# Attention by two problems side by side instead of one, in an eight-core layer kernel

## What is computed

```python
xn = _layernorm(x, axis=-1)                       # x: (4, 4096, 1024)
# attention: b, s, d = 4, 4096, 1024; H = 16, head size 64
Q = (x @ Wq.T).reshape(H, b, s, dkh)              # the same for K and V
scores = jnp.einsum('hbqd,hbkd->hbqk', Q, K)
atten = jax.nn.softmax(scores, axis=-1)
out = jnp.einsum('hbqk,hbkd->hbqd', atten, V).reshape(b, s, -1)
y = out + x
mu, var = mean and variance of y over (1, 2)      # one pair per batch entry
return (y - mu) / jnp.sqrt(var + EPS)
# mixture of experts on xn: gates are the softmax of the two best of 8 logits
h = xt @ w_in[e].T
y = y + gates[:, e:e + 1] * (h @ w_out[e].T)
# result: x + attention(xn) + experts(xn)
```

## Time and profile before

| quantity | value |
|---|---|
| profiled execution | 5827.74 us |
| span of its slowest core | 5825.9 us |
| all cores | 5811.5 to 5825.9 us |
| PE (TensorE) busy | 4843.9 us, 83% |
| ACT (ScalarE) busy | 2392.6 us, 41% |
| DVE (VectorE) busy | 1389.9 us, 24% |
| POOL busy | 146.4 us, 3% |
| mean granted TensorE clock | 0.864 of 2.4 GHz, the same on all cores |
| chain that ended last | PE 67%, ACT 16%, issue 6%, DMA 5%, DVE 5% |

### The profile page before, as it was taken

The page is one execution under the profiler, slowest core; times in us unless marked ns, Lnnn a source line. Parts: engine busy times, 40 slices in busy tenths (PEclk is TensorE's granted clock), DMA queues, the critical chain, the costliest instruction groups (busy, mean ns, idle before and its releaser), DMA issues.

```text
span 5825.9 us, 62049 instructions; the slowest of 8 cores (5811.5 to 5825.9 us)
## 1 busy us (share of the span) xinstructions
PE 4843.9 (83%) x19844; PEld 1763.2 (30%) x19844; DVE 1389.9 (24%) x3688; ACT 2392.6 (41%) x2339; POOL 146.4 (3%) x290
## 2 busy tenths in 40 slices
PE   1888888888888984888888888888968999999994
PEld 1422222232222113222222222222113444444442
DVE  3211111111111105111111111111024444444445
ACT  1455555565555552555556555555530000000000
POOL 1000000000000000000000000000000000000000
PEclk9988888888898556888898889887559999999997
DMA  5000000000000002000000000000026565677543
GB/s 76 4 1 4 4 1 4 1 4 4 1 4 1 4 1 33 1 4 1 4 1 4 4 1 4 1 4 1 0 40 106 92 93 92 100 116 116 96 81 83
DMA packets 86068, 173.88 MB, mean 30 GB/s; under 512 B 4864, under 2 KB 4864, under 8 KB 85760
## 3 DMA queue, kind: packets, MB, share of 16 engines
q0 software_dynamic: 83456, 161.54, 17.8%
q1 hardware_dynamic: 2304, 8.39, 0.4%
HBM read 323.06 MB, written 8.39 MB: 57 GB/s over the span
## 4 chain that ended last, share of the span: by engine, by line
PE 67%; ACT 16%; issue 6%; DMA 5%; DVE 5%; DVEq 1%; ACTq 1%; POOL 0%; POOLq 0%
PE P_OT L374 17%; PE P_S L426 17%; ACT AR L303 14%; PE P_S L504 11%; PE P_A L352 5%; PE P_B L352 5%; PE P_OT L522 4%; DMA AR<-woutT 4%; PE P_B L522 2%; PE P_A L522 2%; PE P_B L361 1%; DMA xstg<-xb 1%; ACT AR L315 1%; PE P_A L361 1%; DVE gsc L623 1%
## 5 line engine op out<-in xcount | busy, mean ns | idle before, releaser
L303 ACT ACTIVATE AR<-P_S,consts 128x1024 bf16<-128x1024 f32 x2048 | 2254.1, 1114 | 1629.3 <-PE P_S L426 1613.2
L374 PE MATMUL P_OT<-AR 128*65 128x512 bf16 x4096 | 1414.0, 430 | 350.9 <-ACT AR L303 350.6
L426 PE MATMUL P_S<-AR 64*128 64x512 bf16 x4096 | 1452.4, 447 | 3.6 <-DVE AR L547 3.0
L504 PE MATMUL P_S<-AR 128*128 128x512 bf16 x4096 | 891.7, 380 | 19.1 <-DMA AR<-woutT 12.9
L374 PEld LDWEIGHTS P_OT<-AR 128*65 128x65 bf16 x4096 | 312.1, 116 | 1304.0 <-issue 1294.7
L504 PEld LDWEIGHTS P_S<-AR 128*128 128x128 bf16 x4096 | 400.6, 98 | 508.6 <-issue 31.7
L426 PEld LDWEIGHTS P_S<-AR 64*128 64x128 bf16 x4096 | 263.2, 99 | 943.5 <-issue 929.5
L734 DVE TENSOR_TENSOR AR<-P_S,AR 128x512 bf16<-128x512 f32 x384 | 265.6, 692 | 412.5 <-PE P_S L504 412.5
L538 DVE CAST AR<-P_B 64x256 bf16<-64x256 f32 x256 | 106.7, 417 | 978.3 <-PE P_B L352 978.3
L538 DVE CAST AR<-P_A 64x256 bf16<-64x256 f32 x256 | 106.6, 417 | 966.4 <-PE P_A L352 966.4
L352 PE MATMUL P_A<-xnTb,AR 128*64 128x256 bf16 x2048 | 319.0, 308 | 1.3 <-DVE xnTb L586 1.3
(11 more groups left out here) (98 smaller groups left out, 1667.8 us busy)
## 6 DMA issues: line engine op xcount, KB each, us to landing
AR<-winN POOLq DMA_DIRECT2D x64, 1024.0 KB, 15.5
AR<-woutT POOLq DMA_DIRECT2D x64, 1024.0 KB, 24.8
xstg<-xb POOLq DMA_DIRECT2D x80, 256.0 KB, 4.8
out<-AR SPq DMA_DIRECT2D x16, 512.0 KB, 3.0
AR<-wqT POOLq DMA_DIRECT2D x2, 1024.0 KB, 14.5
AR<-wkT POOLq DMA_DIRECT2D x2, 1024.0 KB, 25.5
AR<-wvT POOLq DMA_DIRECT2D x2, 1024.0 KB, 36.3
identsb<-idin POOLq DMA_DIRECT2D x1, 32.0 KB, 2.2
```

Source lines behind the costliest of these rows:

```text
L303: inst = ac.activation(AR[:, R_PT + ((k // 2) % 2) * 1024: R_PT + ((k // 2) % 2 + 1) * 1024], pS0[:, sl4 * 512: (sl4 + 2) * 512], AF.Exp, ...
L374: last = pe.matmul(pOT[0:65, (qc % 2) * 512: (qc % 2) * 512 + 512], lhs, rhs, start=(k == 0), stop=(k == 31))
L426: last = pe.matmul(BK[sb][0:128, 0:512], lhs, rhs, start=True, stop=True)
L504: last = pe.matmul(BK[bk][:, 0:512], lhs, rhs, start=(kt == 0), stop=(kt == 7))
```

## The change

Two problems, A and B, are worked on side by side (a pair). Each has two score banks of its own (`P_S0` and `P_S1`, 1024 wide), one half of `R_PT` and one bank of `P_OT`. At each step of two key blocks TensorE takes A's block, then B's. A chunk is now the same chunk of A and of B, so a half has 4 pairs of 8 chunk pairs, with 32 exponentials in each. At the end of a chunk pair there are two copies out and eight transposes.

The groups of the next two problems are dealt as 64 QK groups, 8 to a chunk pair, at every second step; the 8 V groups follow behind the last transposes of the pair. The first pair of each half has its 72 groups ahead of it, and the last pair has none to deal. Q and K of every second pair lie in partitions 64 to 127 of the same columns (`rh`), those of the others in 0 to 63. The sums of y and y*y are taken after every chunk, over 128x128 twice (`stats_part`), behind the norm steps of A and again behind those of B. The rows of x for the residual are laid out for both problems at the start of a pair.

```diff
-BANKS4 = ("S0a", "S0b", "S0c", "S0d")
+BANKS4 = ("S0a", "S0b", "S1a", "S1b")
...
# ScalarE
-            for pj in range(8 * half, 8 * half + 8):
-                for qc in range(8):
-                    for k in range(0, 32, 2):
...
+            for p in range(4):
+                pjA, pjB = first + 2 * p, first + 2 * p + 1
+                for sq in range(8):
+                    for kp in range(16):
+                        for xi, pj in enumerate((pjA, pjB)):
+                            k0 = 2 * kp
+                            W(ac, ("st", pj, sq, k0))
+                            W(ac, ("st", pj, sq, k0 + 1))
+                            if k0 >= 2:
+                                W(ac, ("av", pj, sq, k0 - 1))
...
+                    for xi, pj in enumerate((pjA, pjB)):
+                        W(ac, ("av", pj, sq, 31))
+                        if sq > 0:
+                            W(ac, ("atr", pj, sq - 1, 3))
+                        ac.drain()
+                        inc(ac.copy(
...
# TensorE
-                for qc in range(8):
-                    dealt = 0
-                    for k in range(4):
-                        st_step(pj, qc, k, True)
-                    for k in range(0, 32, 2):
-                        if dealt < DEAL_CNT[qc] and bgi < len(bg) \
-                                and k in DEAL_SLOTS:
-                            pe_qkv_group(*bg[bgi])
...
+                rh = (p % 2) * 64
+                rh2 = 64 - rh
...
+                for sq in range(8):
+                    deals = pref[sq * 8: sq * 8 + 8]
+                    di = 0
+                    for kp in range(16):
+                        if kp % 2 == 1 and di < len(deals):
+                            pe_qkv_group(deals[di][0], deals[di][1], rh2)
+                            di += 1
+                        k0 = 2 * kp
+                        for xi, pj in enumerate((pjA, pjB)):
+                            if k0 >= 2:
+                                av_step(pj, xi, sq, k0 - 2)
+                                av_step(pj, xi, sq, k0 - 1)
+                            st_step(pj, xi, sq, k0, rh)
+                            st_step(pj, xi, sq, k0 + 1, rh)
+                    for xi, pj in enumerate((pjA, pjB)):
+                        av_step(pj, xi, sq, 30)
+                        av_step(pj, xi, sq, 31)
...
+                if p < 3:
+                    for pj2 in (pjA + 2, pjB + 2):
+                        for g in range(32, 36):
+                            pe_qkv_group(pj2, g, 0)
...
# VectorE
+        def stats_part(pj, xi, sq):
...
+            for th in range(2):
...
+                dv.reduce_sum(gsc[:, 7:8], srcv, axis=AXX)
+                dv.drain()
+                dv.tensor_add(stats[:, 0:1], stats[:, 0:1], gsc[:, 7:8])
+                dv.drain()
+                dv.tensor_mul(AR[:, R_YSCR + 512: R_YSCR + 640], srcv, srcv)
+                dv.drain()
+                dv.reduce_sum(gsc[:, 7:8],
+                              AR[:, R_YSCR + 512: R_YSCR + 640], axis=AXX)
```

More of the change, by code:

```diff
@@ L31 @@
 R_XNAT = 37920
-R_YSCR = 39968
+R_YSCR = 52288
 R_OSTG = 34848
@@ L66, in _g_decode, with _pref_list @@
     return 2, g - 32
+def _pref_list(pA, pB):
+    return ([(pA, g) for g in range(32)] + [(pB, g) for g in range(32)])
 def _ab_schedule():
@@ L285, in emit_act @@
         ac.wait_ge(S["sGP"], 1)
[L286 to L290, removed]
         for half in range(2):
+            if half == 1:
+                W(ac, ("outse", 6, 7))
+                W(ac, ("outse", 7, 7))
             act_phase0(16 * half)
-            for pj in range(8 * half, 8 * half + 8):
-                for qc in range(8):
-                    for k in range(0, 32, 2):
[L297 to L319, removed]
@@ new lines, in emit_act @@
+            first = 8 * half
+            for p in range(4):
+                pjA, pjB = first + 2 * p, first + 2 * p + 1
+                for sq in range(8):
[6 more added lines that the diff above has]
+                                W(ac, ("av", pj, sq, k0 - 1))
+                            elif sq > 0:
+                                W(ac, ("av", pj, sq - 1, 31))
+                            elif pj >= 2:
+                                W(ac, ("av", pj - 2, 7, 31))
+                            stb = pS0 if xi == 0 else pS1
+                            inst = ac.activation(
+                                AR[:, R_PT + xi * 1024:
+                                   R_PT + (xi + 1) * 1024],
+                                stb[:, 0:1024], AF.Exp, bias=consts[:, 0:1])
+                            inc(inst, "sAC", ("exp", pj, sq, k0))
+                    for xi, pj in enumerate((pjA, pjB)):
[4 more added lines that the diff above has]
+                        inc(ac.copy(
+                            AR[0:65, R_OUTS + xi * 512:
+                               R_OUTS + xi * 512 + 512],
+                            pOT[0:65, xi * 512: xi * 512 + 512]),
+                            "sAC", ("outse", pj, sq))
@@ L351, in pe_qkv_group @@
                     rhs = xnTb[:, kt * 2048 + toff: kt * 2048 + toff + 256]
-                    last = pe.matmul(BK[bk][0:64, 0:256], lhs, rhs,
-                                     start=(kt == 0), stop=(kt == 7))
+                    last = pe.matmul(BK[bk][rh:rh + 64, 0:256], lhs, rhs,
+                                     start=(kt == 0), stop=(kt == 7),
+                                     tile_position=tp)
             else:
@@ L659, in emit_dve @@
+        alias(("statsall",), ("statsacc", NP - 1, 7, 1))
+        alias(("statslast",), ("statsacc", NP - 1, 7, 1))
         W(dv, ("sum2",))
```

282 lines of the change are left out of this document (144 added, 138 removed).

## The result

The changed kernel takes 5888.9 us (median; the profiled execution 5887.3) against 5842.3 before. Their ratio is 1.0092 with the interval 1.0069 to 1.0116: about 0.9% slower, where I had forecast 5784 and faster.

What follows compares the result with a forecast made beforehand. Neither TensorE nor ScalarE was full; they wait for each other, and TensorE sets the pace at 1.2 GHz. Per half 1391.4 + 558.6 + 35 - 4.4 = 1980.6 against 2002.4 us; two halves save 43.6 from 5827.7: 5784 us, range 5705 to 5905.

Steps and rivals of the forecast that it cites:

- Stream: Exponentials of a chunk pair: same loop as before, 15 x 2.54 + 2.23 = 40.3 us, no gain.
- groups: QK groups ahead of A's block, partly in TensorE's wait: 0.66 us each, 8 per chunk pair, 5.3 us.
- turn: Between chunk pairs, with A's sums (3.0 us) on the path: 9.4 us, against two of 4.62; no gain.
- Restart: Start of the stream after a turn, at 1.2 GHz: third exponential 0.4 to 1.4 us late, taken as 0.9 per chunk pair.
- rival of the late clock: After a turn only the second QK group lifts the clock: 2.7 us x 48 = 131, 5915 us; chance 0.16.
- Last pair: No groups dealt, 1.2 GHz: 71.1 us per chunk pair, the first 50.6 where the clock holds; 558.6 us per half.
- V groups: Behind each of three pairs per half: 16.6 us together with ScalarE idle, the next chunk pair's restart not paid again.
- Groups ahead of the half: 36 more groups before each half's first scores: 35 us more per half.
- Long sums: Sums in the turn take 3.8 us, not 3.0: 64 turns grow by 0.8, +51, 5835 us; chance 0.17.
- cheap ends: Sums 2.4 us (-38), restart 0.4 (-24), last pairs of both halves start at 2.4 GHz (-20): 5702 us; chance 0.17.
- Upper half of the partitions: Scores from partitions 64 to 127 cost 0.05 us more, 2048 of them: +102, 5886 us; chance 0.06.
- Last pair at 2.4 GHz: Both last pairs run at 2.4 GHz, 8 x 50.6 = 405 us each: -308, 5476 us; chance 0.02.

Runs made afterwards that it cites:

- fastest version: Two filler groups, at steps 3 and 5 of each chunk pair of the last pair, added to the kernel with the turn taken apart: 5033.2 us, 0.8624 of before.

## Why the prediction was wrong

- **Stream, groups, turn.** Right: two exponentials in 2.54 us (392.80 to 395.34) and in 3.16 with a group (395.34 to 398.50), turns of 9.4 and 9.7. The sums are 3.1 us against 3.0. The edit that moved the sums measured the same 3.1.
- **Restart.** This step failed. I took 0.9 us for every warm chunk pair, from ends of 0.4 and 1.4 that both assume that the clock is back by A's block behind the first group. Against 55.0 for the rest, the short kind pays 1.3 us and the long kind 4.7, 2.9 in the mean. That is 2.0 us too little in 42 chunk pairs (those with V groups stand below): 84 us. It was my rival of the late clock, priced at 2.7 us and measured at 3.4 (59.7 - 56.3), but in every second chunk pair only. I had argued against it that the first group comes sooner, and for it that the idle turn is twice as long; I let the first weigh more, and put nothing of the second into the sum. The run with the turn taken apart (46.8 us at 1.00, though its first group stands late) shows that this idling is what has to be made good, and the one with the turn filled (54.5) agrees. I also set the margin too wide: no change, by my own 29 us, begins at (5799 - 5784) / 48 = 0.3 us of extra loss per warm chunk pair, not 0.6.
- **Last pair.** The step was right, 71.0 to 71.3 against 71.1. Its start was not: on the slowest core the clock fell 2.6 us behind the first exponential in half 0 and 2.4 in half 1, so the first chunk pair also ran at 1.2 GHz. From the copy before it, V groups and chunk pair together took 87.4, where I had 60.9 + 16.6 = 77.5: 10 us per half. On four of the eight cores it stayed at 2.4 in half 0 (68.0 us, 19 less), on none in half 1. Since the slowest core is what counts, half a chance for one core was the wrong mean.
- **V groups.** A chunk pair with them took 71.7 to 72.3 us against 72.5: two of them in each half, 1 us per half too much.
- **Groups ahead of the half.** Right: with the ends of the halves I had 71 us for both (twice 35 - 4.4, and 4.7 for each longer last turn), and the starts and the break show 72.
- **Sum.** -43.6 + 84 + 20 - 2 = +58, and the profiled executions differ by +59.6 (5887.3 - 5827.7). Nothing large is left over.
- **Rivals.** Long sums and cheap ends: refuted, by 3.1 us for the sums and 2.9 for the restart. Upper half of the partitions: refuted, since the two kinds take 56.4 and 59.7 us in the upper half and 56.2 and 59.8 in the lower. Last pair at 2.4 GHz: not in this kernel (0.50); it does occur once the turn is taken apart.

On the size of short operations: a 128-column reduction took 0.29 us. The Trainium skill, VectorE: DVE Perf Modes, in the section on the TRN2 errata, gives 58 cycles in its table as the fixed part, by which I had worked out 0.19; the trace disagrees. The same section says below the table that this row under-predicts and that the measured fixed part is about 150 cycles; by that, an estimate, a 128-column reduction takes (150 + 128) / 0.96 GHz = 0.29 us, and the trace agrees. I had used the row and passed over its correction.

On the clock: in the last pair of the run with the turn taken apart TensorE was busy 62.88 of 62.88 us at 0.50, chunk pair after chunk pair. The Trainium skill, TensorE: Matmul & The Clock Gate, Part 1, says that sustained activity releases the throttle; by that rule this pair would have taken 42 us per chunk pair. The trace disagrees for this stream, which on other cores ran at 1.00 with the same instructions; in the run with fillers in the last pair, chunk pairs with two more groups read 0.90.

**Open.** Why the clock falls sooner in every second turn, and in which last pairs it falls in the stream, is not settled; the runs show only what shifts the odds (place of groups, length of the turn, fillers). Fillers at the pair boundary of the fastest version were not tried.

## What to carry to other kernels

When two chains are joined to fill each other's waits, look at what they still do one after the other: here the turn stayed whole, and its price is the idle time plus the slow clock behind it. Read the granted clock behind each idle stretch over several repeats, not in one, and ask what dense work stands first behind it. Count what the joined order needs ahead of its start, too: 36 more groups per half cost 72 us here, where the pairing saved 1.8 us per chunk pair. Writing the next chunk's first scores ahead of the transposes, with the sums moved behind them, saved another 11.1 (57.9 to 46.8) in each chunk pair inside a pair.

## What the hardware showed that I had not expected

- More work made the kernel faster: 1,536 unused matmuls in the turns took it from 5887 to 5554 us.
- One and the same stream runs steadily at either level, 41.9 or 62.9 us per chunk pair, to the end of a last pair, and whether the clock falls shows within 3 us of its first exponential.
- The clock can fall in the stream, with TensorE busy 57.58 of 58.00 us behind the fall, and not only in an idle turn.
- An idle turn of the same length (9.4 to 9.9 us) leaves the clock down for very different times: about 10 or 20 us per chunk pair (1 - 0.91 and 1 - 0.83, twice that share of 56 and 60 us).
